# An audio-tower kernel on one core: late expert weights loaded from the loop's last turns, pad rows released by their own count, and the first tile's loads and sums waited for apart

## The reference

```
h = tok(x)                                    # conv, pool, fft, norm
h = h + attn0(layernorm(h))
h = h + ffn0(layernorm(h))                    # w_q = clip(round(w/mean|w|), -1, 1)*mean|w|
h = h + attn1(layernorm(h))
e = argmax(softmax(layernorm(h) @ router_w + router_b))
h = h + max_prob * (silu(z @ w1[e]) * (z @ w2[e])) @ w3[e]      # z = layernorm(h)
```

## Time and profile before

| | |
|---|---|
| median of 3 runs | 1205.06 us (1203.88 to 1205.45) |
| the profiled execution, its own time | 1207.81 us |
| its span, first to last instruction | 1205.9 us |
| busy: PE, DVE, ACT, POOL | 83%, 66%, 70%, 31% of the span |
| mean granted TensorE clock | 0.947 of full speed |

### The profile page before, as it was taken

The page is one execution under the profiler, slowest core; times in us unless marked ns, Lnnn a source line. Parts: engine busy times, 40 slices in busy tenths (PEclk is TensorE's granted clock), DMA queues, the critical chain, the costliest instruction groups (busy, mean ns, idle before and its releaser), DMA issues. The chain is left out here.

```text
span 1205.9 us, 31213 instructions
## 1 busy us (share of the span) xinstructions
PE 1004.8 (83%) x9406; PEld 761.8 (63%) x9439; DVE 792.0 (66%) x2641; ACT 838.8 (70%) x2673; POOL 368.1 (31%) x1100
## 2 busy tenths in 40 slices
PE   3658988999899999898998999999888541999996
PEld 2436666666666666666666666666666421888885
DVE  2355777777777777777777777777775422555553
ACT  1436888888888888888888888888887420333332
POOL 2012333333333333333333333333332211122222
PEclk9987999999999999999999999999999655999998
DMA  6135111111111111111111111111111007122221
GB/s 217 33 118 156 33 40 39 38 45 38 38 38 55 43 48 38 38 38 38 39 43 38 38 44 49 48 43 38 38 33 33 12 20 212 49 58 56 56 61 39
DMA packets 73487, 65.62 MB, mean 54 GB/s; under 512 B 39341, under 2 KB 63696, under 8 KB 73328
## 3 DMA queue, kind: packets, MB, share of 16 engines
q1 hardware_dynamic: 63232, 46.43, 12.9%
q0 software_dynamic: 4512, 12.52, 3.2%
q10 hardware_dynamic: 5712, 6.29, 1.8%
HBM read 36.57 MB, written 28.95 MB: 54 GB/s over the span
## 5 line engine op out<-in xcount | busy, mean ns | idle before, releaser
L1192 DVE SCALAR_TENSOR_TENSOR conv_lo<-xT_lo,c_taps,conv_lo 128x248 f32<-128x248 f32 x192 | 89.8, 468 | 20.4 <-ACT xT_hi L901 20.4
L1137 ACT ACTIVATE e_tanh<-bank_a 128x512 f32<-128x512 f32 x34 | 20.3, 597 | 93.4 <-PE bank_a L590 93.4
L1087 ACT ACTIVATE p<-bank_b,max 128x62 f32<-128x62 f32 x384 | 81.1, 352 | 0.0
L499 POOL TENSOR_TENSOR var_y<-ssq_y,c_eps 128x1 f32<-128x1 f32 x32 | 6.1, 192 | 235.3 <-ACT f_sq L1057 235.3
L590 PE MATMUL bank_a<-e_xT,w_now 128*128 128x128 f32 x544 | 70.5, 284 | 7.5 <-DVE e_gate L1467 3.4
L590 PEld LDWEIGHTS bank_a<-e_xT,w_now 128*128 128x128 f32 x544 | 64.9, 196 | 16.7 <-issue 11.0
L590 PE MATMUL bank_a<-c_wv,a_xT 64*64 64x384 f32 (+1 forms) x512 | 74.0, 503 | 0.0
L590 PE MATMUL bank_a<-a_xT,c_wq 64*128 64x128 f32 (+1 forms) x512 | 71.7, 282 | 0.0
L1462 DVE COPY w_now<-w_sb 128x512 f32 x34 | 14.5, 427 | 83.9 <-PE bank_a L590 74.6
L590 PE MATMUL bank_a<-a_xT,c_wk 64*128 64x128 f32 (+1 forms) x512 | 69.2, 281 | 0.0
L590 PE MATMUL bank_a<-c_wo,oT 128*128 128x192 f32 x384 | 68.5, 329 | 0.5 <-ACT oT L901 0.4
(11 more groups left out here) (264 smaller groups left out, 3006.7 us busy)
## 6 DMA issues: line engine op xcount, KB each, us to landing
rel_scores<-rel_tok SPq DMA_DIRECT2D x32, 492.0 KB, 2.6
rel_skew<-rel_scores SPq DMA_DIRECT2D x64, 124.0 KB, 3.0
x_tok<-in_x SPq DMA_DIRECT2D x32, 187.5 KB
e_rest<-routed SPq DMA_DIRECT2D x34, 97.0 KB
e_tok<-routed SPq DMA_DIRECT2D x34, 96.0 KB, 1.9
routed<-pad_rows SPq DMA_DIRECT2D x8, 386.0 KB, 2.8
w_sb<-in_w ACTq DMA_DIRECT2D x1, 3072.0 KB, 12.4
w_sb<-in_w ACTq DMA_DIRECT2D x2, 1024.0 KB, 14.7
```

What stands on the lines that cost most here:

```text
L499: pool.tensor_tensor(out=var[k][:, :], in0=ssq[k][:, :], in1=c_eps[:, width:width + 1], op=ALU.mult).then_inc(var_eps[k], 1)
L1087: last = nc.scalar.activation(p1[:, h, 0:T], src[:, at * T:(at + 1) * T], ACT.Exp, bias=max1[:, mx:mx + 1])
L1137: nc.scalar.activation(e_tanh[:, :], pa0[:, :], ACT.Tanh, scale=0.5).then_inc(e_tanhr, 1)
L1192: c.mark(v.scalar_tensor_tensor(conv_lo[:, :, :], xT_lo[:, :, k:k + PAIRS], c_taps[:, 0, k:k + 1], conv_lo[:, :, :], ALU.mult, ALU.add))
```

## The change

The four late weight DMAs are issued by SP, after its part of the loop, on a wait for a_v of all 32 tiles. SP's wait for the scatter of tile 30 is taken out. POOL marks the early experts before it waits for the last scatter. w_t is cut to five loads; ident is counted with x; gamma, beta and rk_feat are counted in w_a. PE has no wait in front of its loop; the waits for w_t stand in the first pointwise product (PE) and the first middle tap (ACT), and DVE's first moments wait for w_a. rk goes through bank b0, and is copied by ACT after the first a_copy_x. The two |w| passes run after ACT's first t_copy_z, and the product that adds them stands ahead of PE's first a_relative.

```diff
-        LOADS_T, LOADS_A, LOADS_F, LOADS_B = 9 * 16, 8 * 16, 5 * 16, 12 * 16
+        LOADS_T, LOADS_A, LOADS_F, LOADS_B = 5 * 16, 11 * 16, 5 * 16, 12 * 16
...
-            sp.dma_start(ident[:, :], ident_in).then_inc(w_t, 16)
+            sp.dma_start(ident[:, :], ident_in).then_inc(x_loaded, 16)
...
-            sp.dma_start(c_feat[:, :], rk_feat).then_inc(w_t, 16)
+            sp.dma_start(c_feat[:, :], rk_feat).then_inc(w_a, 16)
...
+            sp.wait_ge(a_v, 4 * TILES)
+            for e, landed in w_late.items():
+                load_weights(sp, slice(e, e + GE), landed)
             sp.wait_ge(pads_ready, 1)
             sp.wait_ge(pads_placed, 1)
-            sp.wait_ge(r_scattered, 16 * (TILES - 1))
...
-            pool.wait_ge(r_scattered, 16 * TILES)
-            for e, landed in w_late.items():
-                load_weights(pool, slice(e, e + GE), landed)
-            for landed, es in ((w_early, range(EARLY)), *((landed, range(e, e + GE)) for e, landed in w_late.items())):
+            def mark_weights(landed, es):
                 pool.wait_ge(landed, 64)
                 for e in es:
                     pool.tensor_tensor(out=w_spare[:, e:e + 1], in0=half[:, :], in1=half[:, :], op=ALU.add).then_inc(w_ready, 1)
+            mark_weights(w_early, range(EARLY))
+            pool.wait_ge(r_scattered, 16 * TILES)
+            for e, landed in w_late.items():
+                mark_weights(landed, range(e, e + GE))
...
                 pe.wait_ge(w_a, LOADS_A)
                 for hp in range(HP):
-                    last = mm(pa0[:, hp * REL:(hp + 1) * REL], c_wrk[:, hp * P:(hp + 1) * P], c_feat[:, :])
+                    last = mm(pb0[:, hp * REL:(hp + 1) * REL], c_wrk[:, hp * P:(hp + 1) * P], c_feat[:, :])
                 last.then_inc(rk_done, 1)
+            def sum_weights():
+                pe.wait_ge(rk_stored, 1)
                 pe.wait_ge(wabs, 2)
                 pe.wait_ge(cleared, 3)
                 mm(pf0[:, 0:2], ones[:, :], wsum[:, :]).then_inc(wtotal, 1)
-                pe.wait_ge(rk_stored, 1)
             def t_transpose(m):
-                pe.wait_ge(x_loaded, 16 * m + 16)
+                pe.wait_ge(x_loaded, 16 * m + 32)
...
             def t_pointwise(m):
+                if first(m):
+                    pe.wait_ge(w_t, LOADS_T)
                 pe.wait_ge(t_conv, m + 1)
...
             def a_relative(m):
+                if first(m):
+                    sum_weights()
                 pe.wait_ge(a_kr, m + 1)
...
-            pe.wait_ge(w_t, LOADS_T)
             overlapped(pe, (
...
-                copy(rk[:, :, :].rearrange("p h r -> p (h r)"), pa0[:, 0:HP * REL]).then_inc(rk_stored, 1)
+                copy(rk[:, :, :].rearrange("p h r -> p (h r)"), pb0[:, 0:HP * REL]).then_inc(rk_stored, 1)
+            def sum_weights():
                 act.wait_ge(w_f, LOADS_F)
...
             def t_middle_tap(m):
+                if first(m):
+                    act.wait_ge(w_t, LOADS_T)
                 act.wait_ge(t_xpose, m + 1)
...
                 copy(z_sb[:, :], pt[:, 0:D]).then_inc(t_zs, 1)
+                if first(m):
+                    sum_weights()
             def a_copy_x(m):
-                if first(m):
-                    prepare()
                 act.wait_ge(a_xpose, m + 1)
...
                 copy(a_xT[KB:P, 1, :], pa0[0:KB, P:2 * P]).then_inc(a_xTr, 1)
+                if first(m):
+                    prepare()
...
             def t_moments(m):
                 ch["t"].stage("moments", m)
+                if first(m):
+                    dve.wait_ge(w_a, LOADS_A)
                 dve.wait_ge(t_y, m + 1)
```

More of the change, by code:

```diff
@@ L387, in _ @@
             sp.dma_start(c_dft_seq[:, :, :], dft_seq).then_inc(w_t, 16)
-            sp.dma_start(c_gamma[:, :], bass.AP(gamma.tensor, 0, [[0, P], [1, D]])).then_inc(w_t, 16)
-            sp.dma_start(c_beta[:, :], bass.AP(beta.tensor, 0, [[0, P], [1, D]])).then_inc(w_t, 16)
-            sp.dma_start(c_feat[:, :], rk_feat).then_inc(w_t, 16)
+            sp.dma_start(c_gamma[:, :], bass.AP(gamma.tensor, 0, [[0, P], [1, D]])).then_inc(w_a, 16)
+            sp.dma_start(c_beta[:, :], bass.AP(beta.tensor, 0, [[0, P], [1, D]])).then_inc(w_a, 16)
+            sp.dma_start(c_feat[:, :], rk_feat).then_inc(w_a, 16)
             sp.dma_start(c_wrk[:, :], wrk).then_inc(w_a, 16)
```

## The result

| | before | after |
|---|---|---|
| median | 1204.47 us (1203.44 to 1205.45, 4 runs) | 1188.28 us (1187.74 to 1189.37, 4 runs) |
| the profiled execution, its own time | 1207.81 us | 1188.7 us |
| its span | 1205.9 us | 1186.9 us |

The ratio is 0.9865, 95% interval 0.9852 to 0.9879: 16.2 us (14.6 to 17.8), where 16.15 were forecast. The changed kernel was timed again in two later sets, in which the kernel before took 1208.6 and 1203.5 us: 0.9878 (0.986 to 0.9896) and 0.9865 (0.985 to 0.988).

A forecast was written before the change was run, and what follows sets the result against it. Both ends bound what the change can bring: PE's early waits, and the hand-over's wait for tile 30 and slow e_tok. 5.0 + 3.75 + 7.4 = 16.15 us off 1205.06 gives 1188.9, range 1184.9 to 1196.3.

The forecast's parts named there:

- Start: Kernel start: tile 0's a_in transposes begin at about 28.39 and not 33.35, 5.0 us gained in all.
- The step on the table load: ACT's first tap: the table load stands behind the new w_t wait, so ACT starts at 8.65, 1.55 us gained.
- |w| passes hidden: Start, on ACT: the moved passes end at 25.8, 2 us ahead of a_in; uncovered they would cost up to 2.86.
- Pads: Hand-over: without the wait for tile 30's scatter, SP issues the first pad at 989.30; all shifts by 3.75 us.
- e_tok: Hand-over: with the late weights moved away, the first e_tok lands in 1.9 us and not 9.3, 7.4 us gained.
- the other cause: Rival at the hand-over: the first e_tok is slow for another reason, 7.4 us stay lost, 1196.3; chance 0.09.
- Tile 30's scatter held by the pads: Rival at the hand-over: the pads hold that scatter by 7.4 us, costing 4.5, 1193.4; chance 0.08.
- a sign that the prediction had named for being wrong: Hand-over: the prediction is wrong if moe_row of tile 31 waits for a scatter; no size given.
- The weights hinder turns 33 and 34: Rival in the last turns: the late weights slow them by up to 7.4 us, 1196.3; chance 0.08.
- The start's gain doesn't get through: Rival in an early turn: it waits for something with a fixed time, such as a load, 1193.9; chance 0.05.
- The clock falls otherwise: Rival in the experts: the higher clock level comes a step sooner or later, 2.7 us, 1186.2 or 1191.6; chance 0.07.
- Slower by the clock: Rival in the full turns: a fall to 1.2 GHz in each of 25 looped turns eats the 16.15; chance 0.02.

The follow-up runs named there:

- after_third: The changed kernel as it is, timed once more as the mark of the third set: 1187.22 us, ratio 0.9865 to the kernel before.
- pads_wait_back: The changed kernel with SP's wait for tile 30's scatter put back in front of the pads: 1195.5 us, ratio 0.9885 to the kernel before.
- pads_two_queues: The changed kernel with the pads of experts 4 to 7 issued by ACT ahead of tile 31's moe_row: 1188.7 us, ratio 0.9878 to the kernel before.
- taps_with_x: The changed kernel with taps counted with x and ident, no w_t wait before ACT's tap: 1192.37 us, ratio 0.986 to the kernel before.
- pads_only: The kernel before without SP's wait for the scatter of tile 30, nothing else changed: 1204.19 us, ratio 0.9972.
- late_weights_only: The kernel before with the four late loads on SP and POOL's marks as in the changed kernel: 1197.89 us, ratio 0.9914.
- weights_after_etok: The kernel before, POOL marking early experts at once and issuing the late weights once the first e_tok has landed: 1206.77 us, ratio 0.998.
- start_only: The kernel before with the start's part of the change alone, late weights and pads as before: 1202.62 us, ratio 0.9967.
- w_t_split_only: The kernel before with w_t cut to five loads, its waits behind PE's transposes, rk through bank b0; |w| passes unmoved: 1203.14 us, ratio 0.9996.
- after_again: The changed kernel as it is, timed again as the mark of the second set: 1193.36 us, ratio 0.9878 to the kernel before.
- sums_only: The kernel before with only the |w| passes, their adding product and rk's copy moved; w_t still waited for whole: 1204.68 us, ratio 0.9967.

## Why the prediction was right, and where its terms were off

**The total.** That the sum came within 0.1 us is in part luck. The terms as measured below give 5.4 + 3.1 + 7.3 = 15.8 us, and the interval of the measured gain is 14.6 to 17.8.

**Start, 5.0 us forecast.** At the transposes four profiles with the start as before give 33.35, 32.98, 32.67 and 33.43, mean 33.11; six with the changed one give 27.83 to 28.36, mean 28.11: 5.0 us. The first tap gives 1.7 of them by the means of the same profiles (9.96 and 8.26), 2.2 in the first pair, and the sums 3.3.

The step on the table load needs mending, though: the prediction's 1.55 us came out nearly right by two errors that offset each other. I took the load to stand behind the wait for w_t, which I put at 7.32, and ACT to start 1.28 us later. The load ran at 6.68, behind the wait for PE's transposes, which came first since x had landed at 5.5; and w_t landed at 3.43 + 4.4 = 7.83. So the two overlap: ACT started at 7.98, not at 8.65. In the six profiles with the changed start w_t lands between 7.83 and 8.43, and the tap follows within 0.3 us; in three of them (after_third, pads_wait_back, pads_two_queues) ACT idles after the table load until c_dft_seq has landed. It is that landing, and hardly the load, that sets the tap.

The Trainium skill (ScalarE: Activation LUTs, "Step-by-step: what each stage is for") says that the compiler puts the load right before the ACTIVATE. This run agrees, 6.68 to 7.96 with the tap at 7.98. In the kernel before, too, no instruction of ACT stands between them, but the load ran at 0.71, 9.5 us ahead of the tap. There one wait stood in front of the ACTIVATE. In all profiles with one wait the load stands at 0.7, in all with two at 6.3 to 7.2, and taps_with_x takes the second wait away from the changed kernel.

At pads_at the same profiles give means of 987.66 and 982.25, 5.4 us. Some 6.5 in the first pair of profiles was partly the luck of one run: tile 0's rel_skew was waited for 0.69 us and not 1.65.

**|w| passes hidden, right.** They ended at 25.5, 1.8 us ahead of a_in; the adding product and rk's copy cost nothing on the path.

**Pads, 3.75 forecast, 3.1 measured** (2.7 to 3.5 by the table); this term was 0.6 too large. Two things shrink it. The first pad goes out 1.49 us after pads_at, not 1.08, in every kernel that has the late weights on SP and no wait for the scatter, while pads_only has the 1.08. The delay comes with the late weights on SP and not with the missing wait: where the wait stands, the first pad goes out 5.3 us after the start of pads_at's row in late_weights_only and pads_wait_back, and 4.9 to 5.1 us in the others. Why was not tried. And the last pad takes 0.2 us longer to land.

**e_tok, 7.4 forecast, 7.33 measured.** late_weights_only is the test, weights_after_etok excludes the other cause. It took 9.3 us beside the weights, 2.0 without, and 2.0 with the weights issued just behind it. The Trainium skill (DMA: Bandwidth & Descriptors, "Queues, rings and completion order") says that a DMA engine takes turns between queues, packet by packet. The estimate that the prediction drew from this, a loss of about e_tok's own 1.9 us, is refuted; the rule itself is neither shown nor refuted. Turns of unequal size alone don't account for the loss, if the packets that the profile counts are those of the turns. Between 1008 and 1021 us of the kernel before the weights' queue moved 2.79 MB in 728 packets, 3.8 KB each, and e_tok's 0.10 MB in 144, 0.7 KB each. One packet of weights ahead of each of its own is 0.55 MB, by estimate 2.0 us at the 270 GB/s of that time, not 7.4. In which order the engines did take the packets was not looked into.

**The rivals.** *Tile 30's scatter held by the pads* came true in its mechanism: 4.85 us in place of 2.74. By a sign that the prediction had named for being wrong, that tile 31's moe_row waits for a scatter, it was wrong here: ACT idled 5.4 us until the scatter had landed. But it cost nothing: the held landing set moe_row 1.3 us later against pads_at, within the slack that the prediction named, since the scatter of tile 31 waits for the pads until 995.2, and DVE's row was ready at 993.0. *The weights hinder turns 33 and 34*: PE waited 0.45 us for rel_skew, and pads_at lost nothing. *The start's gain doesn't get through*: it does, in all profiles and in start_only. But its two halves were not both seen in medians (w_t_split_only). *The clock falls otherwise*: not in this pair, where the first expert step takes 7.22 us before and 7.21 after, at a granted clock near 0.5 both times. *Slower by the clock*: the full turns keep it, 1.00 in the window of the earlier trace rows after as before.

**The parts add up.** 0.33% + 0.86% + 0.28% alone are 1.47%, and 1.35% together (1.21 to 1.48), so no interaction shows; with 0.14 to 0.19 to either side on each part, a small one wouldn't.

## What to carry to other kernels

When a transfer takes five times its usual time, look for what is issued in the same microseconds, and move that to a stretch where the DMA engines are idle, not merely behind the victim, or the next one pays. A wait put in for order's sake should name the thing that is needed (here pads_at), and what the released transfers collide with has to be checked against its slack. When loads are split over semaphores, count what the first instruction needs with what it waits for anyway: here a second wait in front of the first ACTIVATE moved its table load from 0.7 to behind the first wait, where only the other wait's late landing hid it.

## What the runs showed that I had not expected

The eight pads are as heavy as the late weights (3.1 MB) and take 12 us at some 280 GB/s, whether one queue or two issue them; zeroing fewer rows should shorten the hand-over, which was not tried.

A step of the experts takes 4.90 us, but now and then 5.47. Of the 32 steps between the second and the last transposes, such ones number none in the first profile of the changed kernel and in after_third, three in after_again and six in taps_with_x, so that from the first expert transposes to the end it takes 183.6, 182.9, 185.2 and 187.6 us. Two starts of that step in taps_with_x, 5.47 us apart:

```profile
1064.31 0.44 PE L596 MATMUL bank_t<-ident,e_tok 128*128 128x128 f32 x2
1069.78 0.44 PE L596 MATMUL bank_t<-ident,e_tok 128*128 128x128 f32 x2
```

This moves a run by up to 3.4 us with the same work. A microsecond won at the start, as in taps_with_x, drowns in it: its experts begin 2.5 us before those of after_again, and its span is 0.1 us shorter. The count goes with the set more than with the kernel: none in any of the third set's four profiles, three to six in the second's (sums_only has five, pads_wait_back six), two, two, four and seven in the first's. So the sets differ in it, as they do in the time of the kernel before; what in them decides between the two lengths was not looked into.

It also explains the rest of the 19.0 us between the first two profiles. Of the 2.1 us behind the first expert transposes, 1.1 are in the steps, of which the kernel before has two long ones. The other 1.0 is in PE's last products, eight of one kind that took 2.57 us there and 1.56 in the changed kernel. Neither is the change's work.
